# Tree feed-forward stage: leaf rows gathered by index instead of computed for every leaf

## What is computed

```python
logits = x @ W_in.T + b_in                       # x: layer norm of the 2048 tokens, width 8 * 255
decisions = logits > 0
acts = silu(logits)
# from the root, each token goes left or right in each tree by its decisions: 8 nodes are visited
masked = acts * dmap                             # dmap is 1 at the visited nodes, else 0
out = masked @ W_out.T                           # 8 * 255 -> 256 columns
```

## Time and profile before

| what | value |
|---|---|
| median of three runs | 1639.69 us |
| the profiled execution's own time | 1637.88 us |
| its span, first to last instruction | 1636.2 us |
| tree stage, first logits matmul to last add to x | 71.5 to 311.2 us |
| TensorE, VectorE, ScalarE, GpSimd busy over the span | 88%, 66%, 46%, 7% |
| mean granted TensorE clock | 0.953 of full speed |

### The profile page before, as it was taken

How to read it: one execution, slowest core, us unless ns; L and a number is a source line. 1 busy time by engine, 2 the same in 40 slices (tenths; PEclk the granted TensorE clock), 3 DMA queues, 4 the chain that set the end, 5 groups by cost and what they waited for, 6 DMA issues and landing times.

```text
span 1636.2 us, 26350 instructions
## 1 busy us (share of the span) xinstructions
PE 1437.3 (88%) x9842; PEld 1075.0 (66%) x9849; DVE 1073.6 (66%) x2358; ACT 755.9 (46%) x1264; POOL 116.6 (7%) x168
## 2 busy tenths in 40 slices
PE   7999999878887995799888999999997889999557
PEld 5666666557783443477786878787773677788446
DVE  4455675778877874688856464555548988886344
ACT  2212211257773665476662222222224877788323
POOL 1000000000000000111000000000010011001323
PEclk9999999999998997899989999999998999999779
DMA  9462201320000000000009910000100000000166
GB/s 328 166 201 78 78 2 76 143 68 14 13 3 1 1 1 1 24 14 5 10 2 297 284 28 1 1 1 0 33 7 7 1 7 2 7 28 27 41 183 182
DMA packets 60285, 96.62 MB, mean 59 GB/s; under 512 B 11091, under 2 KB 48972, under 8 KB 59982
## 3 DMA queue, kind: packets, MB, share of 16 engines
q1 hardware_dynamic: 57742, 78.50, 15.0%
q10 hardware_dynamic: 544, 12.16, 2.2%
q0 software_dynamic: 1872, 4.27, 0.7%
HBM read 73.21 MB, written 37.30 MB: 68 GB/s over the span
## 4 chain that ended last, share of the span: by engine, by line
PE 52%; issue 18%; DVE 15%; ACT 6%; DVEq 4%; DMA 2%; SPq 1%; POOL 1%; ACTq 1%; POOLq 1%
PE bank L1995 9%; PE bank L1996 9%; PE bank L1687 7%; PE bank L1665 7%; DVE MB L919 3%; PE bank L1792 3%; DVE plo L937 2%; PE bank L1843 2%; PE bank L1593 1%; PE bank L1796 1%; PE bank L1797 1%; PE bank L1763 1%; DMA jx<-copy_routed 1%; PE bank L1765 1%; PE bank L1725 1%
## 5 line engine op out<-in xcount | busy, mean ns | idle before, releaser
L937 DVE TENSOR_TENSOR plo<-e,phi 120x512 f16<-120x512 f32 x256 | 180.2, 709 | 51.4 <-ACT phi L1417 47.7
L1411 ACT ACTIVATE e<-bank 120x512 f32<-120x512 f32 x256 | 150.6, 588 | 41.0 <-PE bank L1797 31.8
L1417 ACT ACTIVATE phi<-e 120x512 f16<-120x512 f32 x256 | 161.2, 630 | 8.8
L919 DVE TENSOR_REDUCE MB<-bank 128x4 bf16<-128x480 f32 x256 | 155.8, 648 | 13.5 <-PE bank L1765 10.3
L1342 ACT ACTIVATE act<-bank,bin 127x512 f32<-127x512 f32 x64 | 43.1, 687 | 167.2 <-DVE dec L757 163.2
L1665 PE MATMUL bank<-xT,winT 128*127 128x512 f32 (+1 forms) x256 | 114.6, 593 | 1.3 <-ACTq L1313 1.3
L1687 PE MATMUL bank<-woutT,msk 128*128 128x256 f32 (+1 forms) x512 | 115.2, 379 | 0.0
L676 DVE TENSOR_SCALAR high<-raw 128x512 int32<-128x512 int32 x96 | 41.0, 427 | 111.8 <-ACT raw L1546 60.8
L1687 PEld LDWEIGHTS bank<-woutT,msk 128*128 128x128 f32 (+1 forms) x512 | 96.9, 190 | 15.4
L556 POOL TENSOR_TENSOR veps<-mv,ceps 128x4 f32<-128x4 f32 x32 | 8.9, 278 | 1342.6 <-DVEq L647 1210.8
L1995 PE MATMUL bank<-hah,h1w 128*128 128x512 f32 x256 | 101.3, 396 | 3.6 <-DVE hal L679 3.6
(11 more groups left out here) (308 smaller groups left out, 3520.9 us busy)
## 6 DMA issues: line engine op xcount, KB each, us to landing
copy_routed<-zeros SPq DMA_DIRECT2D x1, 17028.0 KB
jw<-copy_experts SPq DMA_DIRECT2D x23, 385.0 KB, 3.4
seen<-in_h1T SPq DMA_DIRECT2D x8, 512.0 KB, 7.4
seen<-in_h2T SPq DMA_DIRECT2D x8, 512.0 KB, 4.9
h1w<-copy_h1T SPq DMA_DIRECT2D x1, 4096.0 KB, 17.0
h2w<-copy_h2T SPq DMA_DIRECT2D x1, 4096.0 KB, 15.1
ctxp<-in_ctxT SPq DMA_DIRECT2D x13, 240.0 KB, 3.0
jx<-copy_routed SPq DMA_DIRECT2D x23, 132.0 KB, 3.5
```

The lines of the kernel that those rows point to most:

```text
L919: dve.tensor_reduce(MB[:, t, h0 // 8, SK + h0 % 8:SK + h0 % 8 + 4], b[:, 0:4 * SK].rearrange("p (h k) -> p h k", h=4), AX.X, ALU.max).then ...
L937: dve.tensor_tensor(plo[:, g % 3, :], e32[:, g % 3, :], phi[:, g % 3, :], ALU.subtract).then_inc(s.lo, 1)
L1411: act.activation(e32[:, g % 3, :], bank[2 + g % 3][0:SK, :], ACT.Exp).then_inc(s.exp, 1)
L1417: act.activation(phi[:, g % 3, :], e32[:, g % 3, :], ACT.Copy).then_inc(s.phi, 1)
```

## The change

Steps are now counted over all pairs, `g = 8 * pair + tree`, 32 of them. The leaves' part of the forest is taken out of the matmuls. A table in DRAM holds one row of 513 floats (2052 bytes) for each of 8 x 128 leaves: its row of W_out, its row of W_in, its bias. For each token and tree the number of its leaf is found, that row is gathered, and VectorE makes the dot product with the token's normalised row and adds Silu of it times the W_out row to x. Two buffers of the normalised rows are kept. TensorE's inner part stays, with half the matmuls on each of L1665 and L1687.

```diff
+STEPS, ROW, GB, LAG = PAIRS * TREES, 2 * D + 1, 3, 4
     # SyncE: the W_out part of the table, in place of the load of the leaves' W_out
-        for c, n0, n1 in ((0, 0, 112), (0, 112, INNER), (1, 0, LEAVES)):
+        sp.dma_start(leaves[:, 0:D].rearrange("(t n) d -> n t d", n=LEAVES), nodes[INNER:NODES]).then_inc(leaf_rows, 16)
     # TensorE, first attention, pairs 2 and 3: eight transposes each for the table
+                if i >= 2:
+                    for j in range(2):
+                        for q in range(2):
+                            for k in range(K2):
+                                last = pe.transpose(bank[2 + j][:, ...], winT[:, k, w0:w0 + LEAVES], ident[:])
     # ScalarE: copies them out (2 a pair), then writes the table; the five weight copies go to steps 3, 9, 14, 19, 24
+        act.activation(table[:, :, D], bin2[:, :, 1], ACT.Copy)
+        act.dma_start(leaves[:, D:ROW].rearrange("(t n) c -> n t c", n=LEAVES), table[:]).then_inc(leaf_rows, 16)
     # GpSimd
+        def gather(g):
+            pool.wait_ge(Tf.row, g + 1)
+            if g >= GB:
+                pool.wait_ge(Tf.added, g - GB + 1)
+            for t in range(TT):
+                pool.indirect_dma_start(rowsG[g % GB][:, t, 0:ROW], None, leaves[:],
+                                        bass.IndirectOffsetOnAxis(idx[:, g % TREES, t:t + 1], 0),
+                                        bounds_check=TREES * LEAVES - 1, oob_is_err=False).then_inc(st_job[g % GB], 16)
+        pool.wait_ge(leaf_rows, LEAF_ROWS)
+        for g in range(STEPS):
+            gather(g)
+            if g % TREES == 0:
+                rstd_of(g // TREES + (4 * 1 + 2))
     # VectorE
         def low_bits(i, q):
-            dve.tensor_scalar(seen_low[:], seen[:, q, :].bitcast(I32), 0xFFF, None, ALU.bitwise_and)
-            dve.drain()
-            dve.tensor_reduce(lowmax[:, ds(i * SEEN + q, 1)], seen_low[:], AX.X, ALU.max)
+            dve.tensor_tensor(seen_low[:], seen_low[:], seen[:, q, :].bitcast(I32), ALU.bitwise_or)
+        def leaf_numbers(g):
+            dve.wait_ge(Tf.idx, g + 1)
+            dve.tensor_scalar(idx[:, g % TREES, :], bank[7][:, 0:TT], float(g % TREES * LEAVES), None,
+                              ALU.add).then_inc(Tf.row, 1)
+        def leaf_logits(g):
+            dve.wait_ge(st_job[g % GB], got(g))
+            for t in range(TT):
+                if t == 2:
+                    dve.drain()
+                last = dve.scalar_tensor_tensor(out=dots[:, t % 2, :], in0=rows_in[:, t, :], scalar=1.0,
+                                                in1=rowsG[g % GB][:, t, D:2 * D], op0=ALU.mult, op1=ALU.mult,
+                                                accum_out=lv[:, g % GB, t:t + 1])
+            dve.drain().then_inc(Tf.dot, 1)
+        def add_leaves(g):
+            dve.wait_ge(Tf.val, g + 1)
+            for t in range(TT):
+                last = dve.scalar_tensor_tensor(out=xs, in0=rowsG[g % GB][:, t, 0:D], scalar=val[:, g % GB, t:t + 1],
+                                                in1=xs, op0=ALU.mult, op1=ALU.add)
+            last.then_inc(Tf.added, 1)
+            for g in range(STEPS + LAG + 1):
+                if g < STEPS and (p or not i):
+                    decisions(g)
+                if 1 <= g <= STEPS:
+                    masked(g - 1)                  # inner nodes only
+                if 3 <= g < STEPS + 3:
+                    leaf_logits(g - 3)
+                if 1 <= g <= STEPS:
+                    leaf_numbers(g - 1)
+                if 4 <= g < STEPS + 4:
+                    add_leaves(g - 4)
+                if g < STEPS and not p and i:
+                    decisions(g)
+                if g >= TREES and g % TREES == LAG % TREES:
+                    tree_residual((g - LAG) // TREES - 1)
+                # then as before: p == 1 statistics, p == 3 rows, p == 4, 6 weights;
+                # low_bits at p == 3, 4, 5, 6 one tile each, at p == 7 two
+            dve.tensor_scalar(seen_low[:], seen_low[:], 0xFFF, None, ALU.bitwise_and)
+            dve.drain()
+            dve.tensor_reduce(lowall[:], seen_low[:], AX.X, ALU.max)
     # ScalarE, a step: inner Silu, then 1 at the one leaf, then four Silu of 128 x 1
+        def hot_leaves(g):
+            act.wait_ge(Bf.cnt, g + 1)
+            act.activation(hot[:, g % 2, :], bank[7][:, :], ACT.Relu, bias=onec[:, 0:1]).then_inc(Tf.hot, 1)
+        def leaf_values(g):
+            act.wait_ge(Tf.dot, g + 1)
+            for t in range(TT):
+                last = act.activation(val[:, g % GB, t:t + 1], lv[:, g % GB, t:t + 1], ACT.Silu,
+                                      bias=rowsG[g % GB][:, t, 2 * D:ROW])
     # TensorE, a step: tree_logits(g), right_turns(g - 1), inner_outputs(g - 2), leaf_number(g - 1)
+        def leaf_number(g):
+            pe.wait_ge(Tf.hot, g + 1)
+            for t in range(TT):
+                last = pe.matmul(bank[7][:, t:t + 1], hot[:, g % 2, tok(t)], leafn[:], start=True, stop=True)
+            last.then_inc(Tf.idx, 1)
```

More of the change, by code:

```diff
@@ L142, in build @@
     winT = put("winT", [128, K2, TREES * NODES], F32, at)
[L143 removed]
+    woutT = put("woutT", [128, TREES, D], F32, at)
     end1 = at[0]
+    rowsG = [put("rows0", [128, TT, ROW + 1], F32, at)]
+    xln_odd = put("xln_odd", [128, TT, D], F32, at)
+    assert at[0] <= r1 + 44192
+    table = put("table", [128, TREES, D + 1], F32, [end1])
     at = [r1]
@@ L739, in _, with tree_residual @@
+        def tree_residual(i):
+            dve.wait_ge(Bf.out, i + 1)
+            dve.drain()
+            for h in range(2):
+                residual(i, h, bank[SUMS[i % 2] + h][:, :])
+            dve.drain().then_inc(res_done, 1)
         if phases > 1:
@@ L775, in _ @@
                         low_bits(i, q)
[L776 to L782, removed]
+                    if p == TREES - 1:
+                        dve.drain().then_inc(Ff.low, 1)
+            dve.tensor_scalar(seen_low[:], seen_low[:], 0xFFF, None, ALU.bitwise_and)
+            dve.drain()
+            dve.tensor_reduce(lowall[:], seen_low[:], AX.X, ALU.max)
             dve.drain().then_inc(Ff.low, 1)
@@ new lines, in _ @@
+        if phases > 1:
+            copies = list(w_in.items())
+            for g in range(STEPS + 3):
+                i, p = g // TREES, g % TREES
+                if g in (3, 9, 14, 19, 24):
+                    w, copy = copies[(3, 9, 14, 19, 24).index(g)]
+                    act.dma_start(copy, a[w]).then_inc(w_copied, 16)
+                if i and not p:
+                    evacuate_xT(i + (4 * 1 + 1), 2)
+                if g < STEPS and (p or not i):
+                    inner_values(g)
+                if 1 <= g <= STEPS:
+                    hot_leaves(g - 1)
+                if g < STEPS and not p and i:
+                    inner_values(g)
+                if g >= 3:
+                    leaf_values(g - 3)
@@ new lines, in tree_logits @@
+            def tree_logits(g):
+                i, p = g // TREES, g % TREES
+                if p == 0:
+                    pe.wait_ge(xT_ready, i + (4 + 1))
+                if g >= 2:
+                    pe.wait_ge(Bf.act, g - 1)
+                for k in range(K2):
+                    last = pe.matmul(bank[2 + g % 2][0:INNER, :], winT[:, k, NODES * p:NODES * p + INNER], xT[:, k, :],
+                                     start=(k == 0), stop=(k == K2 - 1))
+                last.then_inc(Bf.logits, 1)
@@ new lines, in inner_outputs @@
+            def inner_outputs(g):
+                i, p = g // TREES, g % TREES
+                if p == 0 and i >= 2:
+                    pe.wait_ge(res_done, i + (4 + 1) - 1)
+                pe.wait_ge(Bf.msk, g + 1)
+                for t in range(TT):
+                    last = pe.matmul(bank[SUMS[i % 2] + t // 2][:, (t % 2) * D:(t % 2) * D + D], msk0[0:INNER, g % 2, tok(t)],
+                                     woutT[0:INNER, p, :], start=(p == 0 and t % 2 == 0),
+                                     stop=(p == TREES - 1), skip_group_check=True)
+                if p == TREES - 1:
+                    last.then_inc(Bf.out, 1)
@@ new lines, in _ @@
+            pe.wait_ge(res_done, 4 + 1)
+            for g in range(STEPS + 4):
+                i, p = g // TREES, g % TREES
+                if g < STEPS and (p or not i):
+                    tree_logits(g)
+                if i and not p:
+                    pe.wait_ge(Bf.act, g)
+                    transpose_rows(i + (4 + 1), 2, (xln, xln_odd)[i % 2])
+                if 1 <= g <= STEPS:
+                    right_turns(g - 1)
+                if 2 <= g < STEPS + 2:
+                    inner_outputs(g - 2)
+                if 1 <= g <= STEPS:
+                    leaf_number(g - 1)
+                if g == 2 * TREES:
+                    pe.wait_ge(wsum, 1)
+                    pe.matmul(bank[7][:, 2 * TT:2 * TT + 2], ones[:], stage_sum[:], start=True, stop=True).then_inc(wsum_ps, 1)
+                if g < STEPS and not p and i:
```

(1 more changed line is left out.)

213 lines of the change are left out of this document (116 added, 97 removed).

## The result

The changed kernel takes 1698.65 us (median of 4 runs, 1694.67 to 1700.33) against 1640.83 (1639.01 to 1646.84) beside it: a ratio of 1.0351, 95% interval [1.0334, 1.0367]. I had forecast 1651.5 and a range to 1684: the sign was right, the size five times too small. The profiled execution took 1699.89 us with a span of 1698.2, which is 62.0 over the span before.

A forecast was written before the change was run, and what follows sets the result against it. VectorE was to bound the tree stage instead of TensorE: 87.5 + (221.4 - 6.9) + 10 + 4 + 6 = 322.0 us against 311.2, +11.8 with the set-up, so 1651.5 us; range 1627 to 1684.

The forecast's parts named there:

- VectorE's work: Tree stage, from the first dot products: 221.4 - 6.9 us of VectorE operations, plus 10 for accumulator outputs.
- stage end: End of the tree stage: 322.0 us instead of 311.2, +10.8.
- the two cases of the accumulator: 128 dot products' accumulator outputs: free as part of the instruction (0 us), or something of their own (10 to 20); 10 taken.
- the end: Last steps of the tree stage: nothing covers the gathers behind the last decisions, 6 us of waiting.
- the set-up: Next layer's set-up: the test's AND and maximum stand ahead of it, half hidden by the mask's arrival, +1 us.
- the start: Tree stage's start: table landed at 79.5 us, four gathers 7.9 us more, so VectorE waits until about 87.5.
- In the middle: Middle steps: a gather of 7.9 us against 8.3 in the tightest step, barely hidden; 4 us of waits (0 to 30).
- My own sign of being wrong: Tree stage: its chain runs through GpSimd or TensorE, or VectorE's start-to-start times differ from those forecast.
- GpSimd or the landing bounds: Rival, tree stage's gathers: issues or landings set the pace; 1664 us at 12 us a gather, middle 1670; chance 0.16.
- its dearer case: Gathers in the tree stage: a row costs two descriptors and 1.94 us to issue, +56 us more than forecast, 1707.
- The clock rival: Rival, tree stage: TensorE, busy 60%, drops to its lower clock; half the steps so +24 us, 1675; chance 0.07.

The follow-up runs named there:

- the traffic off: Changed kernel with weight copies behind the stage, a semaphore for GpSimd's drain, and 18 of 24 low-bit-test tiles loaded only in 16 columns: 1685.32 us.
- the bursts of tiles: Changed kernel with copies in the second cross layer, no drain, and each low-bit-test tile loaded when its buffer is free, not six at once: 1658.77 us.

## Why the prediction was wrong

The sum's own steps, against the profile after, for the stage:

| Step | Forecast, us | Measured |
|---|---|---|
| first dot products | 87.5 | 94.2 |
| VectorE's work behind it | 224.5 (214.5 + 10) | 217.5 |
| waits for rows in the middle | 4 (0 to 30) | 48.3 |
| waits at the end | 6 | 5.6 |
| stage end | 322.0 | 365.6 |

217.5 is 365.6 - 94.2 less the 53.9 us of waits behind the first; 48.3 is these less the last two (1.90 and 3.72).

- **Right: VectorE's work.** 7 us under the sum: the dot products' main part took 0.42, the adds 0.478, the OR 1.224 (I had 1.23 from the two-input row), and each accumulator output has a record of its own of 0.08 us, 128 of them 10.3 us. So I had the right one of the two cases of the accumulator, and the Trainium skill (VectorE: DVE Perf Modes, Two Vector instructions with no wait between them), which has such an operation as two instructions, agrees with these records. The four dot products of a step took 1.76 us with their accumulator reads (94.21 to 95.97), where I had 1.90 and 0.31.
- **Right: the end and the set-up.** 5.6 and 1.2 us (55.6 - 54.4).
- **Off by 6.7: the start.** The table took 7.18 us to land, not 5, and the first gather 10.8 from its first issue (83.44) to the dot product, not 7.9.
- **Failed: "In the middle."** The step read: "It is hidden, but barely ... I put 4 us of waits on that (0 to 30)." The gathers alone bear out that they are just hidden (10.4 us of waits in all with the traffic off). With a slack of 0.4 us the conclusion had to be that every delay of a landing shows in full. I had the transfers (11 MB of copies, 12 MB of tiles) and the row that prices one of them, 20.1 us for h1T, and used it only as a rate for the table. Read as what it is, a stretch of 20 us in which the DMA engines are taken, it gives for two such copies and three of a quarter the size 40 + 15 us of bad time (an estimate) against no slack. The waits measured 48.3 us instead of 4. The experiments put 15 to 19 us to the copies alone (26.4 by the stage end), 33 to copies and drain (36.7), 40 with the bursts of tiles (44.7, from 365.6 to 320.9); that version takes 1658.8 us, and the forecast, which priced none of the three, was 1651.5. My own sign of being wrong, a chain through GpSimd, came: from 60 to 400 us the chain is 18.6% landings of rows and 10.0% GpSimd's issues of gathers, against 14.2% dot products and adds.
- **Missing: the drain.** The prediction moved past it without a word. It stands in the code before, where GpSimd has no DMA outstanding in this stage; the gathers gave it something to wait for.
- **The rivals.** "GpSimd or the landing bounds" (0.16) named the right resource but by another mechanism: it spread a gather of 12 us evenly over the loop of three buffers and had 1664, and its dearer case, issues of 1.94 us, did not come (1.007 in the median). In the trace most gathers landed some 4 us behind their last issue and a few 9 to 13, and VectorE waited for these one by one. The clock rival found its low clock (0.80) and no cost: with the clock still at 0.84 all 40 us came back.
- **Not settled: 6.4 us behind the stage and its set-up.** The first cross layer takes 110.8 us instead of 108.0 at a granted clock of 0.88 instead of 0.91, the second 120.6 instead of 118.7. In the profiled executions of ten of the fifteen variants, not in the changed kernel's, VectorE waits 2.3 to 3.8 us near the end of the last layer (put down to "remote"), at a place that no edit touches. It is a part of why stage ends fell by more than times: without the drain the stage end fell by 14.4 us and that execution by 8.5, with 3.8 in this stall. No run tells where either is from, nor whether the runs without a trace have the stall.

## What to carry to other kernels

Before a step with little slack is made to depend on a small transfer, list every large transfer that can lie beside it and, as a first price, take its whole landing time as time in which the small one may not arrive; an average DMA share tells nothing of that. If small and large must meet, cut the large one into pieces of the small one's size, few at a time, or put it where nobody waits, and look for the next victim there. Here moving the copies gave more at the stage's end (26.4 us) than cutting them (15.6). Whoever gives an engine outstanding DMAs should look through its program for drains.

## What the runs showed of the hardware, unexpected

- A DRAM-to-DRAM copy moved 4.19 MB in packets of 60 KB, 88% of the DMA engines, and beside it a step's last gather took 12.9 us instead of 3.7; behind five such copies (11.5 MB) a 240 KB load took 33.4 us instead of 2.6, and 10.8 when they went in pieces of 2 KB and 1 KB.
- GpSimd's drain behind its gathers lasted up to 16.19 us and ended, at the two places where this could be seen, 0.29 and 1.4 us after VectorE had been let go by the same rows; a semaphore set by the operation before took 0.08.
- ScalarE's DMA issue, 0.5 us, stood up to 18.4 us for two when many small pieces were queued.
- VectorE's two-input operations were not slower beside GpSimd's 128 gathers: the 128 adds took 472 to 493 ns each, whether an issue ran beside them or not, while GpSimd's issues took 992 to 2302 ns, in the median 1007.
- TensorE's granted clock was 0.84 at 174 us busy of 250, and 0.94 at 181 us of 235.5, with identity matmuls added.
